# Message products on 32-column tiles of TensorE, one compare over a whole tile's edges, and a second normalised tile for GpSimd in a graph block with a 30-step scan

## What is computed

```python
xn = layernorm(x)
# graph part: every edge carries a row of xn @ W, scaled, to its destination
agg = segment_sum((xn @ W)[src] * edge_weight[:, None], dst, num_segments=12500)
x = x + relu(agg) + attention(xn)          # attention: folded to one 256 x 256 matrix
# scan part: 30 steps on every row, rows are independent
def step(h):
    h = h + 0.01 * tanh(h)
    h = h * sigmoid(h)
    h = layernorm(h, ln_w, ln_b)
    return h @ W_f.T + b
x = x + scan(step, layernorm(x), 30)
```

## Time and profile before

| | |
|---|---|
| runs | 4112.46 to 4115.05 us, median 4113.03 us |
| profiled execution, first to last instruction (span) | 4114.6 us |
| its own time | not listed apart from the three runs; the span lies between the median and the slowest of them |
| mean granted TensorE clock | 0.996 |
| busy: TensorE, VectorE, ScalarE, GpSimd | 95%, 92%, 84%, 78% |
| DMA | 340 MB, 83 GB/s over the span |

### The profile page before, as it was taken

The page is one execution under the profiler, slowest core; times in us unless marked ns, Lnnn a source line. Parts: engine busy times, 40 slices in busy tenths (PEclk is TensorE's granted clock), DMA queues, the critical chain, the costliest instruction groups (busy, mean ns, idle before and its releaser), DMA issues.

```text
span 4114.6 us, 83954 instructions
## 1 busy us (share of the span) xinstructions
PE 3911.4 (95%) x29240; PEld 3681.5 (89%) x29240; DVE 3767.4 (92%) x7281; ACT 3440.1 (84%) x5133; POOL 3204.4 (78%) x3823
## 2 busy tenths in 40 slices
PE   0899989999999999999999999999999999999999
PEld 0788879999998999999999999999999999899999
DVE  6888779999999999999999999999999999999998
ACT  3333278888888999999899999989999999999998
POOL 4677788888888888888888888888888886555555
PEclk9999999999999999999999999999999999999999
DMA  8555322222223222222322222233222221100000
GB/s 303 163 159 153 110 84 81 77 79 81 77 81 98 82 80 80 76 80 81 99 80 80 75 81 82 75 95 89 75 81 80 76 81 52 52 1 1 1 2 26
DMA packets 215405, 340.39 MB, mean 83 GB/s; under 512 B 79160, under 2 KB 152502, under 8 KB 214994
## 3 DMA queue, kind: packets, MB, share of 16 engines
q0 software_dynamic: 80768, 219.99, 18.7%
q1 hardware_dynamic: 120126, 83.28, 6.9%
q10 hardware_dynamic: 14100, 31.75, 2.3%
HBM read 298.20 MB, written 36.65 MB: 81 GB/s over the span
## 4 chain that ended last, share of the span: by engine, by line
PE 52%; DVE 30%; ACT 9%; POOL 5%; issue 3%; DMA 1%; ACTq 0%; DVEq 0%; SPq 0%; POOLq 0%
PE MM L1439 27%; PE TR L1431 11%; PE AGG L1347 9%; DVE st L1161 7%; DVE v_low L1201 6%; DVE T L1186 6%; ACT T L760 3%; DVE hot L1069 3%; POOL gat_even L562 2%; PE XB L1359 2%; ACT v_high L774 2%; ACT T L765 2%; DVE ve L1166 2%; DVE k_n L1101 1%; POOL rs L536 1%
## 5 line engine op out<-in xcount | busy, mean ns | idle before, releaser
L562 POOL DMA_INDIRECT gat_even<-xn_d,src_cur x1496 | 1495.8, 1000 | 395.7 <-issue 356.2
L1439 PE MATMUL MM<-w_high,v_high 128*128 128x256 f32 x5880 | 1708.4, 291 | 0.0
L1439 PE MATMUL MM<-w_high,v_low 128*128 128x256 f32 x5880 | 1645.5, 280 | 0.0
L1439 PE MATMUL MM<-w_low,v_high 128*128 128x256 f32 x5880 | 1645.2, 280 | 0.0
L1439 PEld LDWEIGHTS MM<-w_low,v_high 128*128 128x128 f32 x5880 | 1114.0, 189 | 0.0
L1439 PEld LDWEIGHTS MM<-w_high,v_high 128*128 128x128 f32 x5880 | 1111.3, 189 | 0.0
L1439 PEld LDWEIGHTS MM<-w_high,v_low 128*128 128x128 f32 x5880 | 1107.1, 188 | 0.0
L765 ACT ACTIVATE T<-T,sh,rs 128x256 f32<-128x256 f32 x2072 | 1093.8, 592 | 2.8 <-DVE sh L1171 2.8
L1161 DVE BATCH_NORM_STATS2 st<-T 128x6 f32<-128x512 f32 x1470 | 968.8, 700 | 124.8 <-ACT T L760 112.3
L774 ACT ACTIVATE v_high<-TR 128x1024 fp32r<-128x1024 f32 (+1 forms) x750 | 757.8, 1010 | 207.6 <-PE TR L1431 197.8
L1201 DVE SCALAR_TENSOR_TENSOR v_low<-TR,v_high 128x1024 fp32r<-128x1024 f32 (+1 forms) x750 | 896.2, 1195 | 25.8 <-ACT v_high L774 24.6
(11 more groups left out here) (189 smaller groups left out, 2669.8 us busy)
## 6 DMA issues: line engine op xcount, KB each, us to landing
gat_even<-xn_d,src_cur POOLq DMA_INDIRECT x1496, 2.8
a_x<-in_x SPq DMA_DIRECT2D x24, 512.0 KB, 7.3
xn_d<-a_x ACTq DMA_DIRECT2D x24, 512.0 KB, 5.5
out_rows<-x_cur SPq DMA_DIRECT2D x23, 512.0 KB
a_x<-xn_d ACTq DMA_DIRECT2D x20, 512.0 KB, 3.9
x_n<-xn_d SPq DMA_DIRECT2D x80, 128.0 KB
x_d<-x SPq DMA_DIRECT2D x80, 128.0 KB
x_cur<-x_d SPq DMA_DIRECT2D x20, 512.0 KB, 3.9
```

The source lines that it names most:

```text
L562: pool.indirect_dma_start(gat[gathered_in(j)][c][:], None, xn_d, bass.IndirectOffsetOnAxis(ap=src_cur[j % 2][:, c:c + 1], axis=0)).then_in ...
L1439: last = mm(MM[b][0:R, t // 2, t % 2 * D:(t % 2 + 1) * D], rows_, w, start=k == 0, stop=k == len(products) - 1)
```

## The change

1. **Edges in order.** The host lays `src`, `dst` and the weights out so that chunk `c` of a node tile is now 128 edges that follow each other. Since edges are sorted by destination, the 32 nodes of *side* `j` can only have edges in the chunks 4j-1 to 4j+4 (six of them, `DEEP`).
2. **Message products.** `g_burst` takes the place of `g_chunk`. For side `j` and each of its six chunks one product with a 128 x 32 stationary matrix and the 128 x 256 gathered rows, put out to PSUM partitions 32j to 32j+31. That is 23 products for a node tile (7 + 8 + 4 + 4 in four *bursts*) in place of 17.
3. **`hot`.** `g_hot` is called once for a node tile: one compare and one multiplication over 4 x 6 x 32 = 768 elements a partition (two `tensor_tensor`), in place of 17 `tensor_scalar` of 128. There are two `hot` buffers.
4. **Gathers** come in the order of the bursts (chunks 3, 7, 11, 15, then 0, 4, ...), as many per slot as before; semaphores count by burst.
5. **Normalisation.** In rounds with messages ScalarE takes two tiles of a unit, GpSimd two.
6. **Start.** Six small indirect DMAs fetch `dst` at the borders between sides, and VectorE tests that every side lies in its six chunks (otherwise the general loop runs); with these inputs all 98 tiles pass. The offsets are ready four groups later.

Core of the diff:

```diff
-HOT_LAG, MUL_LAG = 1, 2
+MUL_LAG = 2
+SCALARS_AT, HOT_AT = (0, 8), (1, 9)
...
-BY_ACT = {True: (0, 1, 2), False: (0, 1)}
-BY_POOL = {True: (3,), False: (2, 3)}
+BY_ACT = {True: (0, 1), False: (0, 1)}
+BY_POOL = {True: (2, 3), False: (2, 3)}
...
-            def g_hot(j, c):
-                if c == 0:
-                    dve.wait_ge(S("edge_scalars_ready"), j * 2 + 2)
-                if j > 0:
-                    dve.wait_ge(S("chunks_multiplied"), (j - 1) * KC + (c + 1))
-                v.tensor_scalar(hot[c][:], iota_f[:], d_loc[:, c:c + 1], w_loc[:, c:c + 1], ALU.is_equal, ALU.mult).then_inc(S("hot_ready"), 1)
+            def g_hot(j):
+
+                e = j % 2
+                dve.wait_ge(S("edge_scalars_ready"), j * 2 + 2)
+                if j >= 2:
+                    dve.wait_ge(S("bursts_multiplied"), bursts_before(j - 1, 0))
+                v.tensor_tensor(hot[e][:], by_pair(d_loc), iota_f[:].rearrange("p (j w) -> p j w", w=WIDE).unsqueeze(2).broadcast_to([128, SIDES, DEEP, WIDE]),
+                                ALU.is_equal).then_inc(S("hot_marked"), 1)
+                dve.wait_ge(S("hot_marked"), j + 1)
+                v.tensor_tensor(hot[e][:], hot[e][:], by_pair(w_loc), ALU.mult).then_inc(S("hot_ready"), 1)
...
-                mm(messages(j), hot[c][:], gat[gathered_in(j)][c][:], start=c == 0, stop=c == KC - 1).then_inc(S("chunks_multiplied"), 1)
+                for d, side, c in BURSTS[g]:
+                    last = mm(messages(j)[side * WIDE:(side + 1) * WIDE], hot[j % 2][:, side, d, :], gat[gathered_in(j)][c][:],
+                              start=(g, d) == FIRST_OF[side], stop=(g, d) == LAST_OF[side])
+                last.then_inc(S("bursts_multiplied"), 1)
```

More of the change, by code:

```diff
@@ L20 @@
 CAP = KC * 128
+WIDE = 32
+SIDES = R // WIDE
+SPAN = KC // SIDES
+DEEP = SPAN + 2
+LAID = -(-(E + CAP + 256) // 128)
+PAST = 1 << 20
+assert SIDES * WIDE == R and SPAN * SIDES + 1 == KC
 QUADS = 5
@@ L59, in grouped, with pairs_of @@
     return [list(range(sum(counts[:k]), sum(counts[:k + 1]))) for k in range(len(counts))]
+GROUPS = [[c for c in range(KC) if c % SPAN == k] for k in (SPAN - 1, *range(SPAN - 1))]
+ORDER = [c for group in GROUPS for c in group]
+GROUP_OF = [g for g, group in enumerate(GROUPS) for c in group]
+def pairs_of(g):
+    return [(d, j, SPAN * j - 1 + d) for d in range(DEEP) for j in range(SIDES) if SPAN * j - 1 + d in GROUPS[g]]
+BURSTS = [pairs_of(g) for g in range(len(GROUPS))]
+FIRST_OF = {j: min((g, d) for g, burst in enumerate(BURSTS) for d, i, c in burst if i == j) for j in range(SIDES)}
+LAST_OF = {j: max((g, d) for g, burst in enumerate(BURSTS) for d, i, c in burst if i == j) for j in range(SIDES)}
+GROUP_ENDS = [max(i for i in range(KC) if GROUP_OF[i] == g) for g in range(len(GROUPS))]
+assert sum(map(len, BURSTS)) == SIDES * DEEP - 1
 LEAD = 6
@@ L88, in early_chunks, with early_bursts @@
     return [divmod(i, KC) for i in range(max(0, (step - LEAD) * PER_STEP), min(limit, (step - LEAD + 1) * PER_STEP))]
+def early_bursts(step):
+    return [(j, GROUP_OF[i]) for j, i in early_chunks(step, MUL_EARLY) if i in GROUP_ENDS]
 def last_step(tile):
@@ L266, in build @@
         w_cur = [sb(f"w_cur{e}", [128, KC]) for e in range(2)]
-        d_loc = sb("d_loc", [128, KC])
-        w_loc = sb("w_loc", [128, KC])
+        d_loc = sb("d_loc", [128, KC + 1])
+        w_loc = sb("w_loc", [128, KC + 1])
         gat = {name: [sb(f"gat_{name}{c}", [128, D]) for c in range(KC)] for name in ("even", "odd")}
-        hot = [sb(f"hot{c}", [128, R]) for c in range(KC)]
+        hot = [sb(f"hot{e}", [128, SIDES, DEEP, WIDE]) for e in range(2)]
         g_x = sb("g_x", [128, D])
@@ L1503, in _ @@
                     f_transpose(0, 0)
-                for j, c in early_chunks(s, MUL_EARLY):
-                    g_chunk(j, c)
+                for j, g in early_bursts(s):
+                    g_burst(j, g)
                 if s < K_TILES:
```

166 lines of the change are left out of this document (100 added, 66 removed).

## The result

The changed kernel takes 4447.51 us (median of four runs, 4445.8 to 4448.67) beside 4114.03 us of the kernel before (four runs): a ratio of 1.081, 95% interval 1.0794 to 1.0825. It is 8.1% slower; 6.6% was forecast. The profiled span grew from 4114.6 to 4445.4 us, by 330.8.

What follows compares the result with a forecast made beforehand. GpSimd was taken as the bound, 72.7 us of a 75.2 us trip, rising to 82.0. Full trips 197, first round 59, early stage 10 and start 3 made +269 us: 4383 us, 6.6% slower, range 4270 to 4475.

Steps and rivals of the forecast that it cites:

- GpSimd is the bound, the gap included: Message rounds: gaps ahead of gathers count as GpSimd's work, giving 72.7 us of a 75.2 us trip.
- rival A: Gaps ahead of gathers are slack that other work can fill; 4015 us, faster; chance 6%.
- Normalisation moved: Full trip: GpSimd gets 15 more tiles at 0.54 us, +8.1 us, with room for 2.5.
- What `hot` does to GpSimd: Message rounds: two-operand VectorE instructions hold GpSimd starts beside them, 0.3 us each, +1.2 us a trip.
- my low end: No stalls, and 1.5 us a trip back from short `hot` no longer disturbing GpSimd: 79.3 a trip, 4270 us.
- Products: TensorE in message rounds: 46 column products overlap two deep, 9.9 us for 14.6, -4.7 us a trip.
- Rival B: Column products on TensorE do not overlap; 83.5 us a trip, 4462 us; chance 10%.
- Early stage and start: Before the rounds: +10 us from 40 new `hot` instructions, +3 us from small gathers and tiny VectorE instructions.
- Trip 39 and the last round: End of the kernel: no messages are made there, so 0 us of change.
- Rival C: Every `hot` instruction holds GpSimd for its whole length, +127 us, 4510 us; chance 7%.
- Rival D: TensorE idles and its clock drops to 1.2 GHz for part of the message rounds; 4500 us; chance 4%.

Runs made afterwards that it cites:

- e2: Kernel before with only the normalisation split changed, two tiles of a unit each for ScalarE and GpSimd; 4344.6 us, ratio 1.056.
- e3: Changed kernel with `hot` made as before, by 17 short `tensor_scalar` a node tile; 4350.4 us, ratio 1.0574.
- e6: Changed kernel with the two `hot` instructions moved behind the statistics and variance of their slot; 4417.7 us, ratio 1.0732.
- e4: Changed kernel with 17 short `hot` and the old normalisation split (ScalarE three tiles, GpSimd one); 4105.3 us, ratio 0.9978 to the kernel before.
- e9: Changed kernel with the second `hot` instruction multiplying by constant 0.5, one SBUF operand for two; 4541.8 us on another chip, ratio 1.0731.
- e10: Changed kernel with the `hot` compare of every node tile issued twice in a row; 4572.6 us on another chip, ratio 1.0816.

## Why the prediction was right, and where it was off

The sign, the engine and the range held; the time was 64 us short, 62 of them in the span. By its steps:

- **GpSimd is the bound, the gap included.** Held. The gaps ahead of gathers are 0.20 and 0.30 us in the rounds of every kernel here, and rival A, which took them for slack, is out. 72.7 us of work in 75.2 was the number that decided, and the busy share of 78% would have hidden it.
- **Normalisation moved**: forecast +5.6 net (8.1 less 2.5 of room), measured +5.9 in a full trip (e2, e3); in the first round +4.7 and +5.4. Its instructions cost what the earlier trace rows said.
- **What `hot` does to GpSimd** is the step that was mis-sized: 1.2 us a trip where 2.2 was measured in the full trips and 2.3 in the first round. (2.2 - 1.2) x 451 / 15 + (2.3 - 1.2) x 140 / 15 is some 40 of the missing 62 us of span. I had the mechanism from the earlier trace rows and then put the instructions at random against GpSimd's starts. They do not stand at random: the order written out puts both of a pair right behind `v_low`, and that is when GpSimd normalises and takes the power, two or three starts in 2 us. Reading one slot's two lists side by side would have given 0.79 + 0.71 for a pair, 3.0 a trip at most, and the pairs do cost 2.9 (e6's section). The 2.2 is that less some 0.6 for the short `hot` that are gone, which my low end had and my sum left out.
- The rest of the 62: 16 from the normalisation's 0.3 and 0.7 us a trip, 3 from counting 29 and 10 trips where 451 and 140 slots are 30.1 and 9.3.
- **Products**: forecast two deep, measured close to four within a burst; by that 46 of them take about 5 us a trip, the low bound. No effect on the total, as forecast, since e2 and e3 have the same trips. Rival B is out. TensorE as a whole came out as forecast all the same, and that was luck: about 69 us a trip was the forecast and 69.3 is measured in e4 (1766 of 1900 us in trips of 74.5), for 74.1 before (from 1400 to 3300 us: 1873). The products gave back more than the 4.7 I had, and the rest of TensorE's busy time grew by what was over; the 0.16 us more that a burst takes and a granted clock of 0.99 for 1.00 are parts of that, and the whole is not accounted for. The Trainium skill (TensorEngine Tiling (Array Packing), Theoretical Speedup) gave up to 4x for 32 columns; with 0.11 us a product for 0.43 the traces here agree.
- **Early stage and start**: 10 + 3 forecast, 12.5 measured. e3's first `h_next` splits it: 588.2 - 583.7 = 4.5 for the start and what is common, 596.2 - 588.2 = 8.0 for the long `hot`, by whatever way; between 460 and 580 us the granted clock fell with them too, from 0.84 in e3 to 0.73.
- **Trip 39 and the last round**: 0 forecast, 0.9 measured.
- **Rival C** (whole length held): a trip would have had 3.8 us for `hot`; 2.2 lies between my 1.2 and that. The Trainium skill (SBUF — State Buffer, Who interferes with whom) says that whoever comes first has the shared ports for its whole instruction and the other blocks fully. Single places agree (1.75 for 1.04), and a line further down is the one that I should have weighed: the order of issue decides who blocks. The same section lists `tensor_scalar` among the operations that can take both port pairs in a fast mode; that fits e9's 0.56 us and its hold, and is the page's reading, since no run here varied the mode alone.
- **Rival D**: the clock did fall. It was granted at 0.97 from 1400 to 3600 us with TensorE 85% busy (1.00 before, 99% busy), and at 0.73 between 460 and 580 (0.90 before), so a part of these stretches ran at 1.2 GHz. It cost nothing that shows: TensorE waits for GpSimd, and e3, with the same products and a clock of 0.98 from 1400 to 3300 us, has the trips of e2 at 1.00.

## What to carry to other kernels

Count an engine's work per repeated unit with the gaps that it can't fill, and compare it with the unit's length: 78% busy was 97% full, and the fifth of free time that the table was meant to fill was not there. Before merging many short VectorE instructions into a few long ones, lay the two engines' lists side by side at the place where they would run: what counts is which GpSimd instruction starts under them. The same two instructions cost 2.9 us a trip beside two tiles and the power, and half of that where they ran two thirds of a slot later. A gain on an engine that shares the bound with two others (here TensorE) is worth nothing until the others are relieved as well; then it was 2.7%.

## What was unexpected of the hardware

- VectorE and GpSimd hold each other both ways, in turn: a compare of 0.95 us took 1.33, a multiplication 2.21 with `g_agg` and `x` of GpSimd passing ahead of it, two normalised tiles 1.88 for 1.09. The Trainium skill's section named above says that the loser blocks fully; it also infers that a `tensor_tensor` doesn't stall the generation of a DMA's descriptors. Here a gather that started 0.17 us into a compare took 1.69 us for 1.04, so the issue of an indirect DMA is held in this case. It reads its row numbers from `src_cur` in SBUF, and no run here tells this read from the generation of descriptors.
- A one-operand instruction over 768 elements took 0.56 us by itself and yet held GpSimd's power by 0.31; an instruction of 1.21 us with one operand in PSUM did not stretch the gather beside it (0.94 us).
- Products on 32 columns overlap close to four deep (four in 0.64 us, eight in 1.07) even when neighbours in the queue share their columns (1.09).
- On the chip of e9 and e10 the kernel before took 4227.68 us for 4114, and the stretch ahead of the first `h_next` over 110 us more than the changed kernel's elsewhere, while the trips were as elsewhere to under 1%. The cause is open.
